# A LayerNorm, banded attention and ternary FFN kernel on eight cores: one head at a time with weights read straight from float32, in place of pairs of heads with weights cast beforehand

## The reference

```python
xn = layernorm(x)                                   # over the last axis, eps 1e-5
q, k, v = xn @ Wq, xn @ Wk, xn @ Wv                 # 16 heads of 128
scores = q k^T / sqrt(128) + mask                   # mask: blocks of 64 tokens, |bi - bj| <= 2
s = softmax(scores) v @ Wo
g = (xn @ gate_w.T) * gate_s
u = (xn @ up_w.T) * up_s                            # inner size 5632
f = ((silu(g) * u) @ down_w.T) * down_s
out = x + s * silu(f)
```

## Time and profile before

| | us |
|---|---|
| two runs of the kernel | 7565.9 and 8538.6, median 8052.25 |
| the profiled execution, its own time | 7489.5 |
| its span, from first to last instruction (slowest core) | 7487.7 |
| spans of the eight cores | 7447.5 to 7487.7 |
| TensorE matmuls busy | 5820.2 (78%) |
| VectorE busy | 1414.6 (19%) |
| ScalarE busy | 905.6 (12%) |
| the 16 DMA engines, ring of SP / ring of POOL | 30.3% / 18.2% of the span |

### The profile page before, as it was taken

How to read it: one execution, slowest core, us unless ns; L and a number is a source line. 1 busy time by engine, 2 the same in 40 slices (tenths; PEclk the granted TensorE clock), 3 DMA queues, 4 the chain that set the end, 5 groups by cost and what they waited for, 6 DMA issues and landing times.

```text
span 7487.7 us, 80845 instructions; the slowest of 8 cores (7447.5 to 7487.7 us)
## 1 busy us (share of the span) xinstructions
PE 5820.2 (78%) x28017; PEld 2702.7 (36%) x28544; DVE 1414.6 (19%) x3939; ACT 905.6 (12%) x2082; POOL 199.1 (3%) x376
## 2 busy tenths in 40 slices
PE   0056307079696999978999888998889998899988
PEld 0023103034342444433444334443334443344433
DVE  0225103023321333321111110111111111111111
ACT  0002102013300333210000000000000000000000
POOL 0000000000000000000000000000000000000000
PEclk9998658589898999989999999999999999999999
DMA  9654994977615765443222443223442224522244
GB/s 118 132 115 133 120 111 73 112 120 184 181 73 124 176 155 136 115 154 107 79 71 65 130 136 95 78 79 113 134 103 79 79 83 134 132 79 73 63 131 127
DMA packets 1121030, 843.22 MB, mean 113 GB/s; under 512 B 570112, under 2 KB 1037056, under 8 KB 1108224
## 3 DMA queue, kind: packets, MB, share of 16 engines
q1 hardware_dynamic: 1076288, 565.39, 30.3%
q0 software_dynamic: 44352, 272.65, 18.2%
HBM read 668.02 MB, written 272.63 MB: 126 GB/s over the span
## 4 chain that ended last, share of the span: by engine, by line
PE 74%; DMA 11%; another core or an unknown queue 7%; DVE 3%; SPq 3%; issue 2%; ACT 1%; DVEq 0%; ACTq 0%; POOLq 0%; POOL 0%
PE pp L705 32%; PE pp L386 12%; PE pp L767 8%; PE pp L775 7%; PE pp L653 6%; PE pp L413 6%; DMA arbf<-dwt 3%; DMA arf<-x 2%; PE pt L559 1%; SPq L465 1%; PE pp L584 1%; SPq L674 1%; DMA wqb<-wq 1%; DMA wkb<-wk 1%
## 5 line engine op out<-in xcount | busy, mean ns | idle before, releaser
L705 PE MATMUL pp<-arbf 128*128 128x512 bf16 x11038 | 2427.9, 380 | 119.2 <-DMA arbf<-uwt 58.1
L386 PE MATMUL pp<-arbf 128*128 128x512 bf16 x3995 | 905.8, 384 | 1075.3 <-DMA arbf<-wkb 609.8
L705 PEld LDWEIGHTS pp<-arbf 128*128 128x128 bf16 x11264 | 1103.8, 98 | 1443.2 <-issue 120.0
L386 PEld LDWEIGHTS pp<-arbf 128*128 128x128 bf16 x4096 | 404.6, 99 | 1558.3 <-issue 1098.8
L767 PE MATMUL pp<-arbf 128*128 128x512 bf16 x3011 | 711.1, 391 | 147.5 <-DMA arbf<-dwt 143.5
L729 DVE SCALAR_TENSOR_TENSOR arbf<-pp,us_sb,arf 128x512 bf16<-128x512 f32 x352 | 264.5, 751 | 2275.9 <-PE pp L705 2275.9
L775 PE MATMUL pp<-arbf 128*128 128x512 bf16 x2509 | 572.6, 380 | 35.2 <-DMA arbf<-dwt 5.7
L722 ACT ACTIVATE arf<-pp,gs_sb 128x512 f32<-128x512 f32 x352 | 241.9, 687 | 2252.3 <-PE pp L705 2252.3
L767 PEld LDWEIGHTS pp<-arbf 128*128 128x128 bf16 x3072 | 306.9, 100 | 534.3 <-issue 194.1
L653 PE MATMUL pp<-arbf 128*128 128x512 bf16 x2006 | 445.0, 382 | 59.6 <-DMA arbf<-ao_h 57.5
L543 ACT ACTIVATE arbf<-arbf,inv 128x384 bf16<-128x384 bf16 (+1 forms) x512 | 278.0, 597 | 1474.1 <-DVE inv L538 1473.8
(11 more groups left out here) (40 smaller groups left out, 1627.8 us busy)
## 6 DMA issues: line engine op xcount, KB each, us to landing
arbf<-gwt SPq DMA_DIRECT2D x352, 256.0 KB, 4.1
arbf<-uwt SPq DMA_DIRECT2D x352, 256.0 KB, 4.1
arbf<-dwt SPq DMA_DIRECT2D x176, 512.0 KB, 6.3
arf<-x SPq DMA_DIRECT2D x32, 1024.0 KB, 6.2
s_h<-arf POOLq DMA_DIRECT2D x32, 1024.0 KB, 4.2
arf<-s_h SPq DMA_DIRECT2D x128, 256.0 KB, 3.5
arf<-x SPq DMA_DIRECT2D x128, 256.0 KB, 3.3
out<-arf POOLq DMA_DIRECT2D x128, 256.0 KB, 2.8
```

The costliest lines, as they stand in the source:

```text
L386: i = e.matmul(pb[:], bf(wsl + 128 * hc, 128), bf(XNT + 2048 * hc + 512 * tc, 512), start=(hc == 0), stop=(hc == 15))
L705: i = e.matmul(pb[:], bf(dstoff + 256 * hc + 128 * sub, 128), bf(XNW + 1024 * hc + 512 * tc, 512), start=(hc == 0), stop=(hc == 15))
```

## The change

- **Weights.** wqb, wkb, wvb and wob and their 16 cast DMAs are gone. The loads of wq, wk, wv and wo slices read the float32 tensors and cast on the way to SBUF; they are issued by POOL and no longer by SP. All of them are done for each of the two sequences. The casts and transposes of gw, uw and dwn stay.
- **Attention.** One head at a time: 16 heads of 19 iterations, `fill(2)` in place of `fill(3)`. Reciprocal and scaling are now in `stageA`, right behind the exponential, and the scaling is a DVE instruction that reads float32 (EB is float32). Transposes, copy and attention times V are one stage, `stageB`, for block j-3. Only head 0 is projected ahead. The background list is served after every fourth filler and twice more for each head, not for each pair: 6 or 7 items a head.
- **P1.** XT and XNB have two separate slots.
- **wo.** Each group of 16 matmuls is cut in four by quarters of AOT and WOS, with a wait for each quarter.
- **P3.** The 16 transposes of 1024 tokens are 32 of 512 tokens, first half first; a group of matmuls waits for its half alone. down_s has its own buffer, loaded at the start.

The diff, cut to its core:

```diff
...
-XNB = (76800, 76800)
+XNB = (68608, 70656)
...
-XT = (0, 0)
+XT = (0, 2048)
+EB = (4096, 4608)
...
-                ops.append(lambda u=u, k=k, wsl=wsl, wnm=wnm: em(
-                    'QS', u, reads=[(wnm, 512 * k, 512 * (k + 1))],
-                    writes=[(RB, wsl + 512 * k,
-                             wsl + 512 * (k + 1))], dma=True))
+                ops.append(lambda u=u, k=k, wsl=wsl: em(
+                    'QG', u, writes=[(RB, wsl + 512 * k,
+                                      wsl + 512 * (k + 1))], dma=True))
...
-            ops += wslice_load(head, wqb, 'wqb', WQS)
-            ops += wslice_load(head, wkb, 'wkb', WKS)
+            ops += wslice_load(head, wq, WQS)
+            ops += wslice_load(head, wk, WKS)
...
-                        in_=wvb[512 * k:512 * (k + 1),
-                                512 * grp_i:512 * (grp_i + 1)].rearrange(
+                        in_=wv[512 * k:512 * (k + 1),
+                               512 * grp_i:512 * (grp_i + 1)].rearrange(
                             "(c p) d -> p c d", p=128))
-                    'QS', u, reads=[('wvb', 512 * k, 512 * (k + 1))],
-                    writes=[(RB, WVS + 2048 * k,
-                             WVS + 2048 * (k + 1))], dma=True))
+                    'QG', u, writes=[(RB, WVS + 2048 * k,
+                                      WVS + 2048 * (k + 1))], dma=True))
...
-                        in_=wob[256 * k:256 * (k + 1), :].rearrange(
+                        in_=wo[256 * k:256 * (k + 1), :].rearrange(
...
                 ops.append(lambda u=u, k=k: em(
-                    'QS', u, reads=[('wob', 256 * k, 256 * (k + 1))],
-                    writes=[(RB, WOS + 4096 * k,
-                             WOS + 4096 * (k + 1))], dma=True))
+                    'QG', u, writes=[(RB, WOS + 4096 * k,
+                                      WOS + 4096 * (k + 1))], dma=True))
...
-            for o in proj_ops(1, seq):
-                o()
-
-            for hp in range(8):
-                heads = (2 * hp, 2 * hp + 1)
-                grp = hp // 2
-                if hp % 2 == 0:
+            for head in range(16):
...
+                base_f = []
+                if head % 4 == 0:
+                    prim_v = vproj_ops(head // 4)
...
-                base_f = []
-                if hp % 2 == 1 and hp < 7:
-                    base_f += wv_load_ops(grp + 1)
-                if hp < 7:
-                    base_f += proj_ops(heads[0] + 2, seq)
-                    base_f += proj_ops(heads[1] + 2, seq)
+                if head % 4 == 3 and head < 15:
+                    base_f += wv_load_ops(head // 4 + 1)
+                if head < 15:
+                    base_f += proj_ops(head + 1, seq)
                 else:
                     base_f += wo_load_ops(seq)
                 fillers = []
...
+                    eb = EB[qb % 2]
+                    em('S', lambda e, pb=pb, W=W, eb=eb, qb=qb: e.activation(
+                        f32(eb, W), pb[:, 0:W], AF.Exp, scale=SCALE,
+                        bias=b12_t[:, 0:1],
+                        accum_out=sums[:, qb % 2:qb % 2 + 1]),
...
+                        writes=[(RF, eb, eb + W), ('sums', qb % 2, qb % 2 + 1)])
+                    em('V', lambda e, qb=qb: e.reciprocal(
+                        inv[:, qb % 2:qb % 2 + 1],
+                        sums[:, qb % 2:qb % 2 + 1]),
+                        reads=[('sums', qb % 2, qb % 2 + 1)],
+                        writes=[('inv', qb % 2, qb % 2 + 1)])
+                    att = ATT[qb % 4]
+                    em('V', lambda e, W=W, eb=eb, att=att, qb=qb:
+                        e.tensor_scalar(bf(att, W), f32(eb, W),
+                                        inv[:, qb % 2:qb % 2 + 1], None,
+                                        op0=ALU.mult),
+                        reads=[(RF, eb, eb + W), ('inv', qb % 2, qb % 2 + 1)],
+
+                def stageB(qb):
+                    att = ATT[qb % 4]
+                    attt = ATTT[qb % 2]
+                    ptb, ptk = PT[qb % 2]
+                    pa, pak = next_bank()
...
-                for j in range(20):
+                for j in range(19):
-                    if 2 <= j < 18:
-                        stageM(heads[0], j - 2)
-                        stageM(heads[1], j - 2)
-                    if 3 <= j < 19:
-                        stageB1(heads[0], j - 3)
-                        stageB1(heads[1], j - 3)
-                    if j >= 4:
-                        stageB2(heads[0], j - 4)
-                        stageB2(heads[1], j - 4)
+                    if j >= 3:
+                        stageB(j - 3)
                     if j < 16:
-                        stageA(heads[0], j)
-                        stageA(heads[1], j)
-                    fill(3)
+                        stageA(j)
+                    fill(2)
...
-                    def womm(e, tt=tt, hc=hc, pb=pb):
-                        for dc in range(16):
-                            i = e.matmul(
-                                pb[:], bf(AOT + 2048 * dc + 128 * tt, 128),
-                                bf(WOS + 2048 * dc + 512 * hc, 512),
-                                start=(dc == 0), stop=(dc == 15))
-                        return i
-                    em('T', womm,
-                       reads=[(RB, AOT, AOT + 32768), (RB, WOS, WOS + 32768)],
-                       writes=[(pk, 0, 1)])
+                    for kq in range(4):
+                        def womm(e, tt=tt, hc=hc, pb=pb, kq=kq):
+                            for dc in range(4 * kq, 4 * kq + 4):
...
+                        em('T', womm,
+                           reads=[(RB, AOT + 8192 * kq, AOT + 8192 * (kq + 1)),
+                                  (RB, WOS + 8192 * kq, WOS + 8192 * (kq + 1))],
+                           writes=[(pk, 0, 1)])
...
+            for half in range(2):
+                for hc in range(16):
+                    em('QS', lambda e, hc=hc, tok0=tok0, half=half:
+                        e.dma_start(
+                            out=bf(XNW + 1024 * hc + 512 * half, 512),
+                            in_=xn_h[tok0 + 512 * half:tok0 + 512 * (half + 1),
+                                     128 * hc:128 * (hc + 1)],
+                            transpose=True),
+                        reads=[('xn_h', tok0 // 128 + 4 * half,
+                                tok0 // 128 + 4 * (half + 1))],
+                        writes=[(RB, XNW + 1024 * hc + 512 * half,
+                                 XNW + 1024 * hc + 512 * (half + 1))],
+                        dma=True)
...
```

More of the change, by code:

```diff
@@ L277, in d2d_cast_unit @@
             return u
-        for r in range(4):
-            units.append([d2d_cast_unit(wo, wob, 'wob', 512 * r, 512)])
         for r in range(8):
@@ L710, in gmm @@
                             return i
+                        xnw_r = [(RB, XNW + 1024 * hc + 512 * tc,
+                                  XNW + 1024 * hc + 512 * (tc + 1))
+                                 for hc in range(16)]
                         em('T', lambda e, gmm=gmm, par=par, pg=pg: gmm(
                             GWS[par], pg, e),
-                            reads=[(RB, GWS[par], GWS[par] + 4096),
-                                   (RB, XNW, XNW + 16384)],
+                            reads=[(RB, GWS[par], GWS[par] + 4096)] + xnw_r,
                             writes=[(pgk, 0, 1)])
@@ L812, in p3_window @@
                         dma=True, lane='bg')
-        for (wsrc, wdst, wnm) in ((wv, wvb, 'wvb'), (wq, wqb, 'wqb'),
-                                  (wk, wkb, 'wkb')):
-            for r in range(4):
-                d2d_cast_unit(wsrc, wdst, wnm, 512 * r, 512)()
         for t in range(16):
```

128 lines of the change are left out of this document (39 added, 89 removed).

## The result

The changed kernel is slower: 1.083 times the kernel before, with a 95% interval of 1.073 to 1.093. The medians of all runs are 9004 us (11 runs, 8128 to 9192) against 7732 us (10 runs, 7492 to 8539). In half or more of the runs of either kernel the cores of one die, or of both, had a lower clock and took longer, so those medians mix two things, while the ratio and all that follows are of executions and dies without that. The forecast was 7990 us with a range of 7600 to 8430: the direction was right, the median lies outside the range, and by ratio 1.056 was forecast where 1.083 came.

The account below looks back on a forecast made before the run. PE was taken to bound P3 and most of the second sequence, with long PE waits in the first; -303, +256, +444 and +28 gave +425, so 7487.7 became 7913, times 1.01 is 7990 us, range 7600 to 8430.

Parts of the forecast that it names:

- a full-speed start at 152: First projection: PE starts at full speed at 152 us instead of 455, -303 us, bounds 130 to 200.
- A closed ring on DVE: Attention iteration without projection: DVE waits for PE and ACT each time, 2.85 us for one head, bounds 1.5 and 3.4.
- I add 4.5 us a head: Attention alone lowers PE's clock: slower products and a 2.8 us restart, 72 us a sequence, bounds 0 and 10 a head.
- First sequence: Casts set the pace from about 480 us, heads 3 to 6 hidden under them; wo ends at 2193 us, before 2240.
- few tens: Sign: PE's waits for wk slices between 500 and 1110 us are a few tens of us, not 540 in all.
- The quarter-wise waits save at most the few us ... I leave them at nothing: wo in quarters: saves at most the few us between first and last load's landing; counted as nothing, wo 219 us.
- half the size may take half or the same ... I take 7: P3: issue of half-size transposes ahead of gate weights costs 7 us a window, bounds 0 and 20, +28 in all.
- rival 1: Not slower: DVE's waits in bare iterations close up to 1.5 us, -405 us, 7508, at run level 7580; chance 0.15.
- rival 2: Slice loads on POOL bind: 15 us for each of 28 heads, +420 us, 8410 us; chance 0.15.
- rival 3: The lower PE clock in attention costs nothing: -130 us, 7860 us; chance 0.1.
- rival 4: Casts don't overlap with the heads, because slices starve behind them: +250 us, 8240 us; chance 0.05.
- I put the forecast at that level: Whole kernel: of earlier runs 7566 and 8539, the lower is 1.01 of profiled time, so 7913 x 1.01 = 7990 us.

Follow-up runs that it names:

- e4: Changed kernel with wo and P3 transposes whole, attention times V one iteration behind its transposes and copy: bare iteration 2.48 us, median span 7577 us.
- e6: Changed kernel with wo and P3 transposes whole, reciprocal and scaling two iterations behind the scores: bare iteration 2.37 us, median span 7831 us.
- e7: Changed kernel with wo and P3 transposes whole, scaling, transposes with copy, and products in three separate iterations: bare iteration 1.55 us, median span 7462 us.
- e1: Changed kernel with each group of 16 wo matmuls in one operation again: median span of cores 4 to 7 8002 us against 8113.
- e2: Changed kernel with 16 P3 transposes of 1024 tokens again: last wo matmul to end 4014.8 us against 4074.6.
- e8: Kernel before with float32 weight loads on POOL and two P1 slots, heads still in pairs: median span 7156 us, ratio 0.958 to before.

## Why the prediction was right and where it failed

**The start, "a full-speed start at 152": mis-sized.** The two groups that need only the first half started at 162.8, but the third only at 188.5, where I had the two done by 159: full speed came about 30 us later. The first sequence as a whole is short by as much (core 6: -16.7 where -47 was forecast). A tile took 6.4 to 7.6 us in the records, near the 6.5 that I took; two of them begin here:

```profile
107.13 2.47 DVE L329 BATCH_NORM_STATS2 bn<-arf 128x6 f32<-128x512 f32 x4 [1.40 <-DMA arf<-x]
...
114.74 2.47 DVE L329 BATCH_NORM_STATS2 bn<-arf 128x6 f32<-128x512 f32 x4 [2.63 <-DMA arf<-x]
```

The term that was off is the 32 transposes, which I took from the earlier trace rows at 54 us. They start at 106, as forecast:

```profile
106.34 77.27 SPq L455 DMA_TRANSPOSE arbf<-xn_h  x32
...
2291.48 69.41 SPq L455 DMA_TRANSPOSE arbf<-xn_h  x32
```

In both places they take longer than the 54 of before. Slice loads run beside them now on the other queue; that these are the reason was not tried.

**"A closed ring on DVE" of 2.85 us, 3.0 with the clock: the mechanism holds, the size was 3.30.** The hand-overs took 0.10 to 0.14 us each and not 0.06; the products took 0.48 us at the lower clock and the output copy began 0.59 after their start, where I had 0.26; the scaling took 0.42 and not 0.25. The links as I listed them add up to 2.61, and the 0.24 us that I added for waits on own results came from no row. That the sum of the second sequence still came within 4 us is luck. Without the wait for the attention output it takes 911 us before (937.6 - 26.6) and 1390 after (1401.0 - 11.4), +479, where I had 1363 - 918 = +445; and that wait went from 26.6 to 11.4, -15, where I had it grow from 28 to 50, +22. The first is 34 too low, the second 37 too high. (The 16 heads were to take 1300 to 1370 us.) e4, e6 and e7 show the ring itself: take one link out and it shortens by that link, from 3.30 to 2.48, 2.37 and 1.55.

**The clock, "I add 4.5 us a head": the level came as forecast, its price isn't known.** It was 0.80 in the second sequence. No run held the clock at full speed with the same order; in e7, with the shorter ring, it was 0.86 from 2400 to 3000 us against 0.80. The 2.8 us that I took for a restart are not what the earlier trace rows show, which is 8.41 - 6.7 = 1.7.

**First sequence: right in its form.** Casts set the pace from about 525 to 1160 us, one per 24 to 33 us where they follow each other, and PE waited 335.9 us in pieces. The longest was 79.8, more than the "few tens" that I named. One cause isn't in the prediction: the fourth load of a head's wq stood behind a store of attention output, which itself was behind casts (POOL's timeline):

```profile
908.58 0.52 POOL L269 DMA_DIRECT2D uwb<-uw  x1 [26.19 <-DMA uwb<-uw]
909.16 0.56 POOL L592 DMA_DIRECT2D ao_h<-arbf  x1
...
910.74 1.49 POOL L354 DMA_DIRECT2D arbf<-wq  x2 [0.17 <-issue]
959.24 0.74 POOL L354 DMA_DIRECT2D arbf<-wq  x1 [47.02 <-DMA ao_h<-arbf]
```

**"The quarter-wise waits save at most the few us ... I leave them at nothing": this step failed.** I asked only what they save, and treated the same 16 matmuls in four operations as the same cost. Three waits of PE on its own semaphore cost 0.9 us a group, 58 us a sequence, and wo as a whole grew by 74, 148 in both; the earlier start gave back 18 or 19 each time (e1). Nothing in my range covered it. `Sync.op` writes such a wait ahead of every quarter but the first of a group; I counted none of them.

**P3, "half the size may take half or the same ... I take 7": mis-sized.** It was the same: 16 to 17 us a window, inside the bounds of 0 and 20, and 43 us more in all than forecast (e2: 60 us given back by undoing it).

**The rivals.** The ring did not close up by itself (rival 1): DVE waits in every bare iteration. But its 1.5 us an iteration is what e7 measured once the stages were moved, 1.55. (Its 7508 us in all lies near the 7462 of e7 by chance: e7 also has the edits of e1 and e2, worth 177 us, which the rival's sum doesn't hold.) The slice loads do not bind outside the casts (rival 2): of 301.2 us of waits for wq on core 6, 299.9 come before 2000 us. That holds as long as the ring is slow; with the shorter iterations of e7 PE waits 61 us for slices of wq and wk in the second sequence. That the clock costs nothing (rival 3) would have made it quicker, and it came slower, but no run tests it. The heads did run under the casts (rival 4): attention of the first sequence ended at 1967 us on core 3, against 1924 forecast and 250 more by the rival.

**The range.** Term by term the shortfall on core 6 is 222 us: 148 in wo, 43 behind it, 30 in the first sequence. Even so the times behind the ratio, 8128 to 8209 us, lie inside 7600 to 8430; the median of all runs, 9004, doesn't. The step that failed there is "I put the forecast at that level", 7913 x 1.01: of the two times that I had, one was 13% above the other, and 8 of the 11 runs of the changed kernel came out at 8530 us or more. The range should have taken in that the median could fall among these.

## What to carry to other kernels

An iteration in which every engine waits for another is as long as the sum of its links, and is shortened by putting another block's work between them, of the same head too (3.30 to 1.55 us here), though the pairs of heads of e8, with the scaling on ACT, stayed 306 us ahead of e7; write out the order on each engine before pricing any single instruction. When one accumulation is cut into several operations, count the waits that each new operation adds on its own engine (three for four pieces here), not only what the finer waits on data may save. A gain ahead of a stage that a transfer paces is worth only what that stage lets through (the slots alone: 55 us at the first matmul of core 6 and nothing at its wo, 50 and 87 at that of two other cores).

## What the runs showed of the hardware

A wait of PE for its own last matmul, between pieces of four matmuls that accumulate into one bank, costs 0.31 us each (0.53 us from start to start where it is 0.22 otherwise); between groups that write different banks nothing is lost. A transposing load of 512 tokens holds SP for 1.18 us in the median and one of 1024 for 1.25, so halving the size nearly doubles the time of issue. POOL took 0.74 us to issue a load of a weight slice, against 0.52 for a cast. A scaling of 384 float32 elements to bf16 took 0.42 us on DVE.
